# Sampled-softmax loss on one core: twofold sampled rows, a new order around the first score, and the last label tile fetched by the sync engine

## What is computed

```python
inputs = front_emb[movie_id[:, 0]]            # 2048 x 64
true_w, true_b = after_emb[labels], after_bias[labels]
samp_w, samp_b = after_emb[sampled_ids], after_bias[sampled_ids]     # 1024 x 64, 1024
true_logits = jnp.sum(inputs * true_w, axis=-1) + true_b
sampled_logits = jnp.einsum('bd,sd->bs', inputs, samp_w) + samp_b
true_logits = true_logits - jnp.log(_log_uniform_expected_count(labels, NUM_SAMPLED, VOCAB))
sampled_logits = sampled_logits - jnp.log(_log_uniform_expected_count(sampled_ids, NUM_SAMPLED, VOCAB))[None, :]
hits = sampled_ids[None, :] == labels[:, None]
sampled_logits = jnp.where(hits, sampled_logits + NEG_INF, sampled_logits)
logits = jnp.concatenate([true_logits[:, None], sampled_logits], axis=1)
loss = jax.nn.logsumexp(logits, axis=1) - logits[:, 0]
```

## Time and profile before

| | us |
|---|---|
| median of 3 runs (61.21 to 62.15) | 61.7 |
| the profiled execution | 60.37 |
| its span, first to last instruction | 58.6 |
| busy: DVE | 47.1 (80%) |
| busy: ACT | 43.2 (74%) |
| busy: POOL | 39.6 (68%) |
| busy: PE | 34.9 (60%) |

### The profile page before, as it was taken

The page is one execution under the profiler, slowest core; times in us unless marked ns, Lnnn a source line. Parts: engine busy times, 40 slices in busy tenths (PEclk is TensorE's granted clock), DMA queues, the critical chain, the costliest instruction groups (busy, mean ns, idle before and its releaser), DMA issues.

```text
span 58.6 us, 616 instructions
## 1 busy us (share of the span) xinstructions
PE 34.9 (60%) x137; PEld 22.6 (39%) x137; DVE 47.1 (80%) x140; ACT 43.2 (74%) x72; POOL 39.6 (68%) x48
## 2 busy tenths in 40 slices
PE   0000184966962679996969786997699949700000
PEld 0000134513610547753747373766375728400000
DVE  3799888899987319999939999999699999990730
ACT  4304999892871039999999799999999995958020
POOL 4076777776777776777777677777776777776000
PEclk9999999999999999999999999999999999999855
DMA  0581111111001110000100000111100111111000
GB/s 0 165 190 40 23 23 37 30 30 23 22 22 32 35 22 22 22 22 22 45 22 22 22 22 23 28 37 34 31 23 23 23 23 46 23 23 23 23 0 6
DMA packets 1715, 1.91 MB, mean 33 GB/s; under 512 B 944, under 2 KB 944, under 8 KB 1712
## 3 DMA queue, kind: packets, MB, share of 16 engines
q0 software_dynamic: 1280, 1.33, 9.5%
q1 hardware_dynamic: 432, 0.55, 3.7%
HBM read 1.87 MB, written 0.01 MB: 32 GB/s over the span
## 4 chain that ended last, share of the span: by engine, by line
ACT 54%; DVE 23%; DMA 7%; PE 7%; issue 4%; SPq 1%; DVEq 0%
ACT psum L329 23%; ACT masks L312 13%; ACT masks L307 11%; DMA sample_ids<-sample_row 7%; DVE wT_low L390 5%; DVE psum L497 5%; ACT xT L325 4%; DVE masks L384 4%; PE psum L276 2%; PE psum L278 2%; PE psum L277 2%; ACT wT_high L319 1%; DVE b_split L398 1%; DVE b_parts L486 1%; DVE b_split L399 1%
## 5 line engine op out<-in xcount | busy, mean ns | idle before, releaser
L497 DVE CUSTOM_DVE_ANT_0 psum<-psum,masks 128x1024 f32<-128x1024 f32 x16 | 19.4, 1226 | 0.1
L218 POOL DMA_INDIRECT t_rows<-after,rows x16 | 15.6, 974 | 4.9 <-issue 4.9
L218 POOL DMA_INDIRECT x_rows<-front,rows x16 | 15.4, 963 | 4.9 <-issue 4.9
L329 ACT ACTIVATE psum<-psum,lowest 128x1024 f32<-128x1024 f32 x16 | 17.2, 1078 | 1.9 <-DVE lowest L497 1.8
L276 PE MATMUL psum<-wT_high,xT 128*128 128x512 f32 x32 | 13.8, 430 | 6.2 <-ACT psum L329 4.1
L278 PE MATMUL psum<-b_parts,ones 128*128 128x512 f32 x32 | 12.7, 396 | 0.0
L277 PE MATMUL psum<-wT_low,xT 128*128 128x512 f32 x32 | 12.6, 394 | 0.0
L307 ACT ACTIVATE masks<-sample_ids,neg_label 128x1024 f32<-128x1024 int32 x8 | 9.2, 1145 | 3.3 <-DMA sample_ids<-sample_row 3.3
L218 POOL DMA_INDIRECT w_rows<-after,rows x8 | 7.7, 967 | 3.8 <-issue 2.1
L276 PEld LDWEIGHTS psum<-wT_high,xT 128*128 128x128 f32 x32 | 6.0, 187 | 10.8 <-issue 7.3
L312 ACT ACTIVATE masks<-masks,ln_big 128x1024 f32<-128x1024 f32 x8 | 9.2, 1150 | 0.1
(11 more groups left out here) (80 smaller groups left out, 34.0 us busy)
## 6 DMA issues: line engine op xcount, KB each, us to landing
sample_ids<-sample_row SPq DMA_DIRECT2D x1, 512.0 KB, 4.1
x_rows<-front,rows POOLq DMA_INDIRECT x16, 2.4
t_rows<-after,rows POOLq DMA_INDIRECT x16, 2.4
w_rows<-after,rows POOLq DMA_INDIRECT x8, 2.4
id_cols<-ids SPq DMA_DIRECT2D x1, 20.0 KB, 1.6
out<-loss SPq DMA_DIRECT2D x1, 8.0 KB, 1.4
```

Source lines behind the costliest of these rows:

```text
L218: return pool.indirect_dma_start(dst, None, table, bass.IndirectOffsetOnAxis(ap=rows[:, col:col + 1], axis=0))
L329: nc.scalar.activation(logits(t), logits(t), ACT.Exp, bias=lowest[:, t:t + 1], scale=-1.0, accum_out=sums[:, t:t + 1]).then_inc(exp_ok, 1)
L497: V.tensor_tensor_reduce(out=logits(t), in0=logits(t), in1=masks[:, t, :], scale=1.0, scalar=3e38, op0=ALU.add, op1=ALU.min, accum_out=low ...
```

## The change

**Twofold rows.** A new table `after_twice` holds the 64 weights twice and then the bias, so a sampled row is 129 floats. `turn_w` turns 128 columns at once, and both halves of wT_high and wT_low come from one instruction each.

**A new order around the first score.** `split_b` is called twice, for three quarters and for the last, and not four times. `turn_x(0)` stands ahead of the last `turn_b`, and `turn_x(1)` ahead of the first score. The upper half of `b_parts` is laid down by ACT and not by DVE. ACT makes the masks of tiles 0, 1, 2, 5, 8, 10, 12 and 14; in the loop it still makes four, and three and one ahead of it, as before. DVE makes four masks ahead of the loop, where it made two.

**The last label tile.** SP loads the 128 label ids of tile 15 in one row (`line_ids`), between `id_cols` and `sample_ids`. DVE turns them into table rows, three instructions on one partition. SP then takes each table row into a register and issues a transfer of that one row, 128 times. POOL leaves this tile out.

**The end.** The last four dot products subtract themselves from `base` and give `gap` at once; the twelve others are subtracted in one instruction ahead of them.

```diff
         def _(sp):
             sp.dma_start(id_cols[:, :], ids).then_inc(ids_in, 16)
+            sp.dma_start(line_ids[:, :], line).then_inc(line_in, 16)
             sp.dma_start(sample_ids[:, :], sample_row.rearrange("(a n) -> a n", a=1).to_broadcast([P, SAMPLES])
                          ).then_inc(row_in, 16)
+            sp.wait_ge(line_rows_ok, 1)
+            for p in range(P):
+                row = sp.value_load(line_rows[0:1, p:p + 1], min_val=0, max_val=VOCAB + SPREAD - 1)
+                sp.dma_start(t_rows[p:p + 1, SP_TILE, :], after[bass.ds(row, 1), :]).then_inc(line_t_in, 16)
             sp.wait_ge(loss_ok, 1)
...
             for j in range(SAMPLE_TILES):
-                gather(w_rows[:, j, :], after, j).then_inc(w_in[j // 2], 16)
+                gather(w_rows[:, j, :], after_twice, j).then_inc(w_in[j // 2], 16)
...
-                    gather(t_rows[:, t, :], after, LAB + t).then_inc(t_in[k], 16)
+                    if t != SP_TILE:
+                        gather(t_rows[:, t, :], after, LAB + t).then_inc(t_in[k], 16)
...
-                nc.scalar.copy(wT_high[0:EMBED, w_cols(q)], psum[0:EMBED, q, 0:2 * P]).then_inc(wT_high_ok, 1)
-                act.wait_ge(wT_high_ok, 2 * q + 1)
-                nc.scalar.copy(wT_high[EMBED:, w_cols(q)], wT_high[0:EMBED, w_cols(q)].bitcast(f32)
-                               ).then_inc(wT_high_ok, 1)
+                nc.scalar.copy(wT_high[:, w_cols(q)], psum[:, q, 0:2 * P]).then_inc(wT_high_ok, 1)
...
+            def split_b(first, last):
+                for q in range(first, last):
+                    dve.wait_ge(w_in[q], 32)
+                tiles = slice(2 * first, 2 * last)
...
+            dve.wait_ge(line_in, 16)
+            dve.wait_ge(line_limits_ok, 1)
+            V.tensor_scalar(line_wrap[:, :], line_ids[:, :], 0.0, float(VOCAB), ALU.is_lt, ALU.mult)
+            link(V.scalar_tensor_tensor(line_low[:, :], line_ids[:, :], float(-VOCAB), line_limits[:, :], ALU.max, ALU.min))
+            V.tensor_tensor(line_rows[:, :], line_low[:, :], line_wrap[:, :], ALU.add).then_inc(line_rows_ok, 1)
...
-                dve.wait_ge(t_in[k], 16 * (b - a))
+                if k == SP_GROUP:
+                    dve.wait_ge(line_t_in, 16 * P)
+                else:
+                    dve.wait_ge(t_in[k], 16 * (b - a))
                 if b - a == 1:
                     V.tensor_tensor_reduce(out=prod[:, a, :], in0=x_rows[:, a, :], in1=t_rows[:, a, :],
-                                           scale=1.0, scalar=0.0, op0=ALU.mult, op1=ALU.add,
-                                           accum_out=dots[:, a:b]).then_inc(dot_ok, 1)
+                                           scale=-1.0, scalar=base[:, a:b], op0=ALU.mult, op1=ALU.add,
+                                           accum_out=gap[:, a:b]).then_inc(gap_ok, 1)
```

More of the change, by code:

```diff
@@ L12 @@
 AUG = EMBED + 1
+TWICE = 2 * EMBED
 SAMPLES = 1024
@@ L23 @@
 SPREAD = P * (CORR + TILES)
+SP_TILE, SP_GROUP = 15, 6
 X_GROUPS = [(0, 1), (1, 2)] + [(t, t + 2) for t in range(2, TILES, 2)]
-ACT_MASKS = (0, 1, 2, 3, 6, 9, 12, 15)
+ACT_MASKS = (0, 1, 2, 5, 8, 10, 12, 14)
+BATCHED = 12
 T_GROUPS = [(0, 4), (4, 8), (8, 12), (12, 13), (13, 14), (14, 15), (15, 16)]
@@ L34, with log_uniform_loss @@
 LN2_LOW, LN2_HIGH = -0.00021219444, 0.6933594
-def log_uniform_loss(nc, ids, sample_row, front, after, out):
+def log_uniform_loss(nc, ids, line, sample_row, front, after, after_twice, out):
     f32, f32r, i32 = mybir.dt.float32, mybir.dt.float32r, mybir.dt.int32
@@ L66, in log_uniform_loss @@
         id_cols = sb("id_cols", [P, COLS], i32)
+        line_ids = sb("line_ids", [1, P], i32)
+        line_wrap = sb("line_wrap", [1, P])
+        line_limits = sb("line_limits", [1, P], i32)
+        line_low = sb("line_low", [1, P])
+        line_rows = sb("line_rows", [1, P], i32)
         limits = sb("limits", [P, COLS], i32)
@@ L75, in log_uniform_loss @@
         ln_big = sb("ln_big", [P, 1])
-        w_rows = sb("w_rows", [P, SAMPLE_TILES, AUG])
+        w_rows = sb("w_rows", [P, SAMPLE_TILES, TWICE + 1])
         x_rows = sb("x_rows", [P, TILES, AUG])
@@ L154, in log_uniform_loss @@
         row_in = sem("row_in")
+        line_in = sem("line_in")
+        line_rows_ok = sem("line_rows_ok")
+        line_t_in = sem("line_t_in")
+        line_limits_ok = sem("line_limits_ok")
         limits_ok = sem("limits_ok")
@@ L188, in log_uniform_loss @@
         dot_ok = sem("dot_ok")
+        gap_ok = sem("gap_ok")
         neg_gap_ok = sem("neg_gap_ok")
@@ L210, in _ @@
             pool.iota(limits[:, :], pattern=[[P, COLS]], base=VOCAB - 1, channel_multiplier=1).then_inc(limits_ok, 1)
+            pool.iota(line_limits[:, :], pattern=[[1, P]], base=VOCAB - 1, channel_multiplier=0).then_inc(line_limits_ok, 1)
             pool.memset(ident[:, :], 0.0).then_inc(ident_zero, 1)
@@ L238, in turn_w @@
                 for i in range(2):
-                    m = nc.tensor.transpose(psum[0:EMBED, q, i * P:(i + 1) * P], w_rows[:, 2 * q + i, 0:EMBED],
-                                            ident[:, :])
+                    m = nc.tensor.transpose(psum[:, q, i * P:(i + 1) * P], w_rows[:, 2 * q + i, 0:TWICE], ident[:, :])
                 m.then_inc(w_turned, 1)
             def turn_b(q):
-                pe.wait_ge(b_split_ok, q + 1)
+                pe.wait_ge(b_split_ok, 1 if q < 3 else 2)
                 for i in range(2):
@@ L287, in _ @@
             turn_b(1)
+            turn_b(2)
             keep_busy(3)
             turn_w(3)
-            turn_b(2)
+            turn_x(0)
             turn_b(3)
-            turn_x(0)
+            turn_x(1)
             for t in range(TILES):
@@ L298, in _ @@
                 if t == 0:
-                    turn_x(1)
                     turn_x(group_of(2))
@@ L345, in _ @@
             raise_w(2)
+            hit(2)
             act.wait_ge(b_turned, 2)
             nc.scalar.copy(b_parts[0:2, 0:BANK], psum[0:2, 4, :]).then_inc(b_low_ok, 1)
-            hit(2)
+            square(5)
             raise_w(3)
             raise_x(0)
+            act.wait_ge(b_turned, QUARTERS)
+            nc.scalar.copy(b_parts[0:2, BANK:], psum[0:2, 5, :]).then_inc(b_high_ok, 1)
             raise_x(1)
+            hit(5)
             raise_x(2)
[L353 to L358, removed]
+            between = {0: (square, 8), 1: (hit, 8), 3: (square, 10), 4: (hit, 10), 6: (square, 12), 7: (hit, 12),
+                       9: (square, 14), 10: (hit, 14)}
             for t in range(TILES):
@@ L387, in lower_w @@
             def lower_w(q):
[L388 to L399, removed]
+                dve.wait_ge(wT_high_ok, q + 1)
+                V.tensor_tensor(wT_low[:, w_cols(q)], psum[:, q, 0:2 * P], wT_high[:, w_cols(q)].bitcast(f32),
+                                ALU.subtract).then_inc(wT_low_ok, 1)
+            def split_b(first, last):
+                for q in range(first, last):
+                    dve.wait_ge(w_in[q], 32)
+                tiles = slice(2 * first, 2 * last)
+                link(V.tensor_tensor(b_cols[:, tiles], log_count[:, tiles], w_rows[:, tiles, TWICE], ALU.subtract))
+                link(V.tensor_copy(b_split[:, tiles, 0], b_cols[:, tiles]))
+                V.tensor_tensor(b_split[:, tiles, 1], b_cols[:, tiles], b_split[:, tiles, 0].bitcast(f32),
                                 ALU.subtract).then_inc(b_split_ok, 1)
@@ L476, in _ @@
             dve.wait_ge(log_count_ok, 1)
-            split_b(0)
-            split_b(1)
+            split_b(0, 3)
+            lower_w(2)
             dve.wait_ge(row_in, 16)
             make_mask(DVE_MASKS[0])
-            lower_w(2)
-            split_b(2)
             make_mask(DVE_MASKS[1])
-            split_b(3)
-            dve.wait_ge(b_turned, QUARTERS)
-            V.tensor_copy(b_parts[0:2, BANK:], psum[0:2, 5, :]).then_inc(b_high_ok, 1)
+            split_b(3, 4)
             lower_w(3)
             lower_x(0)
+            make_mask(DVE_MASKS[2])
             lower_x(1)
+            make_mask(DVE_MASKS[3])
             def mask_and_reduce(t):
@@ L522, in _ @@
                     lower_x(group_of(t + 3))
-                if masks_made < len(DVE_MASKS) and t % 3 != 2:
+                if masks_made < len(DVE_MASKS) and t % 2:
                     make_mask(DVE_MASKS[masks_made])
@@ L532, in _ @@
             link(V.tensor_tensor(base[:, :], base[:, :], log_count[:, SAMPLE_TILES:], ALU.add))
-            for k in range(3, len(T_GROUPS)):
+            dve.wait_ge(dot_ok, BATCHED // 4)
+            V.tensor_tensor(gap[:, 0:BATCHED], base[:, 0:BATCHED], dots[:, 0:BATCHED], ALU.subtract).then_inc(gap_ok, 1)
+            for k in range(BATCHED // 4, len(T_GROUPS)):
                 dot(k)
-            dve.wait_ge(dot_ok, len(T_GROUPS))
-            link(V.tensor_tensor(gap[:, :], base[:, :], dots[:, :], ALU.subtract))
+            dve.wait_ge(gap_ok, 1 + TILES - BATCHED)
```

(4 more changed lines are left out.)

3 lines of the change are left out of this document (1 added, 2 removed).

## The result

The changed kernel takes **171.38 us** (median of 4 runs, 171.2 to 171.41) where the kernel before took 61.56 beside it: ratio 2.806, 95% interval 2.781 to 2.831. Some executions of the kernel before, here and beside the experiments, end at 61.4 to 62.4 us where the others take 60.4 to 61.2, and the ratios leave those slow ones out, so they are not the quotients of the medians. The profiled execution's span is 169.6 us.

A forecast was written before the change was run, and what follows sets the result against it. POOL's gathers were taken as the nearer bound, ACT/DVE ending within 0.6 us of them. Only the 1.31 us of Part 1 counted, all else hidden: 61.7 - 1.3 = 60.4 us, range 59.5 to 72.3.

The forecast's parts named there:

- Part 4: SP's 128 row fetches for tile 15: 0.36 us a row, between 0.25 and 0.55, last row landing at 50.8, hidden.
- 0.387 us a row: SP's row loop: the most each row may cost if the last is to land by 54.25.
- SP's row loop becomes the bound: Rival at SP's queue and DVE's last wait: slower, decided from 0.387 us a row, 81.3 us at the upper end; chance 0.38.
- estimate of some 132 us: SP's row loop if a register load has the skill's floor of some 600 ns: 0.95 us a row.
- Part 1: POOL's gather of tile 15 left out: last landing 1.25 us earlier, tail 0.42 instead of 0.48, gain 1.31 us.
- Part 2: Twofold rows: ACT loses 1.6 us of copies, DVE's subtractions take 1.65 less, POOL's gathers of 516-byte rows cost nothing more.
- longer gathers of `w_rows`: Rival on POOL: twofold rows take twice the time for eight gathers, 68 us; chance 0.05.
- Part 3: Order around the first score: first score at 17.7, not 19.61; ACT's first exponentials about 20.8, 3.4 us earlier.
- 20.8 + 29.9 = 50.7: ACT's loop from first exponentials at its earlier length; `base` there by 51.5, 2 us ahead of 54.10 with 0.5 added.
- The last term: From profiled execution to median: the median 61.7 stands 1.33 us over the profiled execution.

The follow-up runs named there:

- e3_fixed_rows: Changed kernel with SP's 128 row transfers from fixed table rows, without register loads and their arithmetic: 60.37 us, ratio 0.993 to the kernel before.
- e8b_fixed_later: Changed kernel with SP's row transfers from fixed rows, no loads, and the third group of dot products behind the loop: 59.83 us, ratio 0.985.
- e7b_dots_later: Changed kernel with POOL gathering all 16 label tiles again and the third group of dot products behind the loop: 60.89 us, ratio 1.003.

## Why the prediction was wrong

The forecast was 60.4 us, the range 59.5 to 72.3; measured 171.4. **The step that failed is Part 4**, "five steps at 0.05, 0.25 us a row. Upper end: an issue at the full 0.35 and four steps, 0.55". The gap of 0.05 between two issues was made the price of a whole register instruction, for the load too. It is only what lies between instructions: the runs showed 0.48 for the load, 0.15 and 0.04 for arithmetic, 0.02 for the test and 0.03 for a step not counted at all, and then 0.03 to 0.05 between each of the six. The row costs 1.26 us, 2.3 times the upper end. A load into a register was an unknown with no near row, and nothing in the rows gave four such steps an upper end of 0.2 us. The bound that the argument did have, 0.387 us a row, was sound, and the issue alone (0.30 in `e3_fixed_rows`) took three quarters of it: there was room for 0.09 of everything else.

The rival "SP's row loop becomes the bound" named the mechanism, its place and its point of decision; its price, 81.3, was too low by 90 us for the same reason. The estimate of some 132 us, which the Trainium skill's floor for a load gave ("DMA: Bandwidth & Descriptors", latency and other measured facts), was nearer, but not because that floor held: it over-priced the load (0.60 for 0.48) and the transfer (0.35 for 0.27), and left out the arithmetic, the test and the gaps (some 0.5).

**Part 1**, one gather less: right in the gather, wrong in the tail. The last one starts at 51.74, predicted 51.70. From the start of tile 14's dot product to `neg_gap`, `e8b_fixed_later` needs 55.06 - 54.53 = 0.53, and the forecast had 0.42: the new form, which gives `gap` at once, takes 0.28 a piece where the old took 0.23. Against the old 0.48 the tail loses 0.05 and doesn't gain 0.06. From `e7b_dots_later` to `e8b_fixed_later`, where gathers are the last wait on both sides, one gather is worth 60.89 - 59.83 = 1.1 us, predicted 1.31.

**Part 2**, twofold rows cost POOL nothing: right, the gathers of 516-byte rows take 971 ns, those of 260 took 967. The rival of longer gathers of `w_rows` falls. Full height cost DVE no more either: 420 ns for `wT_low`, where half height took 412.

```profile
L237 POOL DMA_INDIRECT w_rows<-after_twice,rows x8 | 7.8, 971 | 3.7 <-issue 2.1
```

**Part 3**, the order around the first score: predicted 17.7 for the first score, measured 17.84; the logarithm of the count was to come 0.6 later and came at 12.14 where it had 11.48; 20.8 for the first exponentials, measured 21.34. ACT's first mask was not put back by 0.43 (5.28, before 5.27): `sample_ids` landed in 3.7 us and not in 4.1. The step from there failed: "20.8 + 29.9 = 50.7" carried the pace of the loop before into a loop that starts 2.8 us earlier, and left out that DVE's dot products stand in the loop and wait for gathers whose times are POOL's: the third group can't start before 50.4. `base` came at 54.5, predicted 51.5, and ACT and DVE ended behind the gather of tile 14 again (51.74 and some 2.5, 54.2). `e7b_dots_later` shows that this one call of `dot` was the cause: with it moved, `base` is ready at 52.7. It did not change the time with 40 gathers, since POOL's last one ends the chain there. So with a row loop that fits, the forecast would have been too low by this step: `e3_fixed_rows`, which has such a loop, has the ratio 0.993, a gain of some 0.4 us and not 1.3. That its 60.37 us look like the forecast's 60.4 is luck: the forecast counted down from 61.7.

**The last term**, 1.33 us from the profiled execution to the median, was carried over from three runs of the kernel before. In the changed kernel it is 0.01 (171.37 and 171.38).

## What to carry to other kernels

Price a loop on a queue by its whole body times its count, and ask first what each iteration may cost; an instruction that the trace doesn't show is to be measured by itself before it is put 128 times in a row, and the gap between two instructions is no price for an instruction. When two chains end within 1% of each other, shortening one gives its gain to waiting; look for where the shortened one meets the other's results ahead of the end, here a group of dot products in the loop, and read the slack there (0.4 us) before counting the gain.

## What was not expected of the hardware

A load into a register on SP takes 0.48 to 0.53 us behind a transfer and 0.27 behind the test of another load. An SP transfer to one partition takes 0.27 us to issue behind register arithmetic and 0.225 to 0.25 behind other transfers (medians), where those to 128 partitions took 0.35 to 0.43. A gather of 80 rows takes POOL 0.91 us; most of those of 128 rows take 0.94, whether a row has 256, 260 or 516 bytes, and single ones up to 1.35.
